# Node-row one-hots of a GNN edge phase: from tensor_scalar to tensor_tensor with a PSUM operand, and behind the copy of places

## The reference, cut to what matters

```python
h = silu(edge_rbf @ W1 + b1)              # per edge, 8 -> 128
weights = h @ W2 + b2                     # per edge, 128 -> 128
node_j = node_feats[col]                  # gather of the neighbour's row
messages = node_j * weights
aggregated = segment_sum(messages, row)   # a later phase here
```

## Time and profile before

| | us |
|---|---|
| median of 3 runs | 8842.73 (8837.77 to 8855.31) |
| the profiled execution | 8818.33 |
| its span on the core | 8816.7 |
| busy: PE / DVE / ACT / POOL | 5016.2 / 3899.3 / 1911.4 / 5309.5 |

### The profile page before, as it was taken

One profiled execution on the slowest core, in us unless ns is written; L12 is line 12 of the kernel. 1 busy time (PEld: TensorE's weight loads), 2 busy tenths in 40 slices (PEclk: granted clock), 3 DMA queues, 4 the chain that ended last, 5 costly groups with the idle time before them and its releaser, 6 DMA issues. The chain is left out here.

```text
span 8816.7 us, 124446 instructions
## 1 busy us (share of the span) xinstructions
PE 5016.2 (57%) x25826; PEld 4198.6 (48%) x25826; DVE 3899.3 (44%) x9651; ACT 1911.4 (22%) x6476; POOL 5309.5 (60%) x5985
## 2 busy tenths in 40 slices
PE   5888888888888888133233332333444444444438
PEld 4777777777777788132222332222322232232234
DVE  6555555555555677233222422232422223223238
ACT  2222222222222001111111111111211212112117
POOL 3556655656656786556666666666366666666651
PEclk7666666666667899566656555555666666666669
DMA  3222222222222686212222122222122222222224
GB/s 104 91 91 95 92 95 91 93 94 95 92 95 93 198 236 211 59 40 47 47 46 47 42 47 47 46 47 47 40 61 59 60 61 59 60 60 60 61 64 155
DMA packets 947475, 711.07 MB, mean 81 GB/s; under 512 B 602499, under 2 KB 811606, under 8 KB 946622
## 3 DMA queue, kind: packets, MB, share of 16 engines
q0 software_dynamic: 163632, 347.28, 13.6%
q1 hardware_dynamic: 245634, 251.14, 9.5%
q10 hardware_dynamic: 538001, 110.77, 6.5%
HBM read 544.79 MB, written 170.29 MB: 81 GB/s over the span
## 5 line engine op out<-in xcount | busy, mean ns | idle before, releaser
L768 POOL DMA_INDIRECT arena<-x1d,edge x3322 | 3148.9, 948 | 1855.5 <-issue 959.2
L1949 PE MATMUL bank<-arena 128*128 x7040 | 1428.4, 381 | 2148.5 <-DVE acc_b L1598 1204.0
L1949 PEld LDWEIGHTS bank<-arena 128*128 128x128 f32 x7040 | 1306.8, 284 | 2338.9 <-issue 2329.0
L707 POOL DMA_INDIRECT msgs<-arena x1664 | 1655.5, 995 | 1242.8 <-DVE arena L1390 764.8
L1592 DVE TENSOR_TENSOR arena<-bank,arena 128x1024 f32<-128x1024 f32 x440 | 537.8, 1223 | 2499.8 <-remote 2090.0
L998 ACT ACTIVATE arena<-edge,arena 128x1 f32 x3520 | 732.0, 282 | 2607.7 <-issue 2057.4
L1598 DVE TENSOR_TENSOR acc_b<-acc_b,bank 128x129 f32 x1760 | 508.5, 289 | 666.1 <-issue 472.2
L1855 PE MATMUL bank<-w2s,acc_b 128*128 128x128 f32 x3328 | 749.9, 394 | 17.0 <-issue 16.5
L1838 PE MATMUL bank<-arena 128*128 (+1 forms) x3328 | 699.6, 363 | 89.3 <-issue 85.1
L1855 PEld LDWEIGHTS bank<-w2s,acc_b 128*128 128x128 f32 x3328 | 636.7, 285 | 161.8 <-issue 161.8
L1838 PEld LDWEIGHTS bank<-arena 128*128 128x128 f32 x3328 | 609.1, 266 | 118.5 <-issue 116.9
(11 more groups left out here) (310 smaller groups left out, 5732.9 us busy)
## 6 DMA issues: line engine op xcount, KB each, us to landing
arena<-rows SPq DMA_DIRECT2D x208, 512.0 KB
arena<-msgs ACTq DMA_DIRECT2D x464, 136.0 KB, 3.3
arena<-msgs SPq DMA_DIRECT2D x464, 136.0 KB, 3.2
arena<-x1d,edge POOLq DMA_INDIRECT x3322
msgs<-arena POOLq DMA_INDIRECT x1664
pred<-arena ACTq DMA_DIRECT2D x98, 256.0 KB
arena<-pred SPq DMA_DIRECT2D x12, 1792.0 KB, 8.8
arena<-xwin SPq DMA_DIRECT2D x208, 64.0 KB
```

The costliest lines, as they stand in the source:

```text
L707: pool.indirect_dma_start(msgs, bass.IndirectOffsetOnAxis(ap=pos[:, b, j:j + 1], axis=0), mrow[:, b, j, :], None).then_inc(scattered[b], 16)
L768: pool.indirect_dma_start(grow_t[:, sl, 0:D], None, x1d, bass.IndirectOffsetOnAxis(ap=edge2[:, odd * RING + sl, 1:2].bitcast(i32), axis=0) ...
L1949: last = mm(sum_at(q, k), oh1[:, q % 2, k, :], grow[:, bass.ds(rows_at[q * TG + k], CW)], start=True, stop=True)
```

## The change

The window one-hots of group g+1 are made by `tensor_tensor` instead of `tensor_scalar`. The second operand is the partition number in one f32 column of PSUM (`number_at`, column 8 of `bank[6]`), broadcast over 8 x 128; it is filled once, ahead of the phase, by a copy of `iota_c`. And the instruction stands behind the copy of places of group g, ahead of the two halves of its messages, no longer between the first scan and the first place product. The first group's one-hots, ahead of the loop, stay where they were.

```diff
-        places_at = bank[6][:, 0:TG]
+        places_at, number_at = bank[6][:, 0:TG], bank[6][:, TG:TG + 1]
...
-                v.tensor_scalar(wsel[:, b], rowsb[:, b, 1, :].rearrange("p (j e) -> p j e", j=TG), iota_c[:, :], None, ALU.is_equal).then_inc(s["wsel_ready"], 1)
+                v.tensor_tensor(wsel[:, b], rowsb[:, b, 1, :].rearrange("p (j e) -> p j e", j=TG),
+                                number_at.rearrange("p (j e) -> p j e", j=1).to_broadcast([P, TG, P]), ALU.is_equal).then_inc(s["wsel_ready"], 1)
...
                     if then:
                         running_counts(ls, 1 - b, 0)
-                        window_onehots(it + b, 1 - b)
                         places_of(ls, g + 1, 1 - b, 0)
...
                     v.tensor_copy(pos[:, b, :], places_at).then_inc(s["pos_ready"], 1)
+                    if then:
+                        window_onehots(it + b, 1 - b)
                     messages(g, b, 0)
...
+            ls.link(v.tensor_copy(number_at, iota_c[:, :]))
             attribute_parts(ls, 0, 0)
```

## The result

The changed kernel took 8939.42 us (median of 4 runs, 8916.06 to 8970.94) against 8840.25 us of the kernel before beside it (4 runs, 8817.72 to 8855.31): a ratio of 1.0116, 95% interval [1.0088, 1.0143], 99 us slower. In a later set of runs (a set is what was measured beside the same executions of the kernel before) the same two kernels took 9001.26 and 8775.11 us, 1.0258 [1.0225, 1.0291]. Slower both times, but the size of the loss differs by a factor of two between the sets. The traces show in which groups the difference lies, and not why.

The account below looks back on a forecast made before the run. Bound: POOL's series of eight scatters plus the path copy, messages, first scatter (13.15 us a group). Only the insertion was priced: 8843 + 118 = 8961 us, other terms nothing; range 8790 to 9200 us.

Parts of the forecast that it names:

- The main step: Edge phase: PE's results come free only when POOL's scatters are through, in almost every group; period 13.15 us.
- first rival: POOL's scatters were held up by the old one-hots; removing them takes 156 us off, to 8805 us; chance 0.21.
- Series plus path: The assumed bound: POOL's eight scatters, 9.97 us, then copy of places, messages and first scatter; sum 13.15 us.
- The form: One-hots on DVE: 756 ns as tensor_scalar become 1.22 us as tensor_tensor with one PSUM operand, bounds 0.76 and 1.4.
- The insertion: One-hots between copy of places and messages: 1.25 us in 5 of 11 groups, 118 us in all; chance 0.52.
- The old place: Between first scan and place product DVE loses 0.76 us per group; nothing gains, as DVE stands 4.0 us anyway.
- PE behind the one-hots: PE's products for the next group start 1 to 2 us later against the messages; costed at nothing.
- SP's queue: Row and attribute loads wait for the later one-hots; DVE may stand up to 2 us at L1375; costed at nothing.
- second rival: PE's answers miss their time and stay held until the series ends: 290 us, 9250 us; chance 0.14.
- POOL's queue: POOL's scatter series: its waits do not change, the series stays 9.97 us; gain 0, at most 54 us.
- The rule that the prediction weighed: On DVE and POOL: 2-port vector instructions and GpSimd exclude each other, normal-mode PSUM ones do not; up to 156 us less.

Follow-up runs that it names:

- c1: The kernel before itself, unchanged, run again for its trace: 8756.3 us, ratio 0.9986 to the kernel before.
- d2: The kernel before plus an idle 1.2 us PSUM-operand comparison behind the copy of places, which then gives the copy's signal: 8895.0 us, ratio 1.0085.
- d1: The changed kernel with the removed tensor_scalar put back idle at its old place; PE still waits for the new one-hots: 9100.7 us, ratio 1.0308.
- c2: The changed kernel itself, run again in a later set: 9001.3 us, ratio 1.0258 to the kernel before.
- e3: The kernel before with only the one-hots' form changed, tensor_tensor with the number from SBUF, at the old place: 7586.5 us, ratio 1.0273.
- c4: The kernel before with its old one-hots one instruction later, behind the first place product: 8744.6 us, ratio 0.9973.
- f1: The kernel before with its one-hots one instruction earlier, ahead of the first scan: 7543.1 us, ratio 1.0208.
- e1: The changed kernel with the one-hots in their old tensor_scalar form, still behind the copy of places: 7479.7 us, ratio 1.0128.

## Why the prediction was right and wrong

The number was right: 8961 us forecast, 8939 measured, period 13.9 forecast and 13.92 in the trace. That it came out so close is luck. The composition was wrong: terms that I had set at nothing were larger than the one I priced, and they partly cancelled. In the later set the same pair lost 226 us, nearly twice the forecast.

- **The main step: PE's results come free when the scatters are through.** The prediction named its own sign of being wrong, results that come free at another time relative to POOL's last scatter, and that sign is there. In the kernel before, the copy of places began 0.99 us behind the end of the series (median; ahead of it in 43 of 207 groups; in c1 0.15 us and 63 groups). In the changed kernel it began 1.90 us ahead of that end, and ahead of it in 130 groups. The messages began 0.99 us behind the end, 1.70 before, and in 65 groups POOL went into the next series after its short pause of 0.30 us, in 18 before. So the first rival's sign (no later than 1.71 us) showed too, though not its cause, since the series had become longer. "Series plus path" describes the kernel before; in the changed one some groups are bound by the series alone and others by PE's late answers.
- **The form.** 1.22 us forecast, 1.212 measured.
- **The insertion**, "mean 5/11 x 1.25 = 0.57 us; over 207 groups 118 us". Mechanism right, size off: 63 us in d2, 0.30 us per group. Part of it is the distance: the one-hots begin 0.08 us behind the copy's start, so the least distance from copy to messages is 1.21 us in the trace, not 1.42. The sample of eleven groups was not at fault. Of all 208 groups of the trace of before, 106 have their messages within 0.25 us of the copy, and raising every distance below 1.21 us to that value adds up to 115 us (96 us in c1). What gave back the rest is not shown.
- **"The old place. Nothing gains."** This failed. That DVE stood 4 us ahead of the copy in the mean does not say that it stood in every group. In the trace of after it went into the copy without a wait (under 0.4 us) in 65 groups, in that of before in 21. Against d1, with the old instruction still there, POOL's idle time is 336 us smaller.
- **"PE behind the one-hots: I cost the shift at nothing under that cover", and "SP's queue: nothing".** Together they failed by 206 us (d1 against d2). The mechanism was in the text as the second rival, at 290 us, with a chance of 0.14; the wait at L1375 had been named, and rose from 65 to 229 us. The rival's sign, copies 17 to 19 us apart, is there: the trace of after has 42 groups with over 17 us between their messages, that of before 16. These groups are also where the two pairs differ: c2 has 71, c1 18.
- **"POOL's queue: the series still 9.97 us."** This failed. I looked at the instruction that is removed and whether it held a scatter. It did not, and the row was no accident: 160 of the 161 scatters that began in it in the trace of before did so in its first 0.1 us, and 159 were let through. Taking it out gained nothing there. I did not look at what its removal does to the instructions behind it. They moved against the scatters, and L707 was busy 206 us longer. The forecast "idle time before the first scatter near 3.7 us" was wrong for the same reason in the other direction: by the group it was 3.13 us before and 2.72 after.

The rule that the prediction weighed (the Trainium skill, SBUF — State Buffer, section "Who interferes with whom") goes on in that section to say that a vector instruction with two SBUF inputs contends with a GpSimd instruction that reads SBUF, and one with at most one such input, outside the 2-port modes, does not. Here the trace agrees on both: scans, products and the one-hots of e3 (two SBUF inputs) held the scatters, 94 of 94 in e3's one-hots; the PSUM form and the messages held 0 of 43 and 0 of 101. The half that the prediction weighed, on tensor_scalar, shows only when a scatter begins well inside the instruction: 116 of 116 in c4, 46 of 46 in f1. I had applied the rule to the moved instruction alone.

Three terms thus make up the changed kernel's loss at this level: the insertion, about 63 us; the late signal, about 206, both measured within one set; and the instruction taken off DVE with the scans' new distance, which together give back between 44 and 170 us. This last is an estimate across sets (1.0308 less 1.0258 or 1.0116, of 8840), because the changed kernel was not measured beside d1 and d2. Why it differs so between two sets of the same kernels stays open.

## What to carry to other kernels

When an instruction leaves a place, ask what its removal does to the timing of the ones that stay, above all where two engines exclude each other and a rhythm happens to fit; the distance between two instructions can be worth more than the instruction. When one that signals is moved, price the signal apart from the work: here the signal's delay cost three times what the added work on the path did (206 us and 63). And a total that comes out right is no proof of the terms; an idle copy of the instruction at the old place and one at the new place, measured beside the change itself, separate most of them.

## What the runs showed of the hardware

**Scatters held by VectorE's instructions.** A GpSimd indirect DMA that begins while VectorE runs a scan ends 0.78 us after it (352 of the 355 that began with over 0.25 us of a scan left, in the changed kernel), in a product or a comparison with both inputs in SBUF 0.84 us after it, and so in the tensor_scalar L1384 when it began more than some 0.1 us into it (116 of 116 in c4). One that began in the first 0.1 us of tensor_scalar was mostly let through (159 of 160 in the trace of before); in the two-input one-hots of e3 0.03 us were enough to be held. VectorE's own instruction is not lengthened: the scans lasted 1271 to 1293 ns in the changed kernel.

**PE's results withheld, in some sets.** The prediction could not say why PE's results came free only behind the scatters. In the sets at 7385 us they do not wait. In e1 ACT evicts the node rows as soon as PE's record ends (1504.37 + 1.92 = 1506.29), in the middle of a series:

```profile
1504.37 1.92 PE L1840 MATMUL bank<-arena 128*128 128x128 f32 x8
...
1505.57 0.97 POOL L707 DMA_INDIRECT msgs<-arena  x1 [0.31 <-issue]
...
1506.40 0.60 ACT L881 ACTIVATE arena<-bank 128x512 f32<-128x512 f32 x1 [0.97 <-PE bank L1840]
1506.52 0.97 PEld L1840 LDWEIGHTS bank<-arena 128*128 128x128 f32 x8
1506.57 1.11 PE L1840 MATMUL bank<-arena 128*128 x8
1506.84 0.97 POOL L707 DMA_INDIRECT msgs<-arena  x1 [0.30 <-issue]
```

The signal of the places comes 0.01 us after the record of their last product there, and 5.4 us after it (median) in the trace of before. It is not the level alone: in the changed kernel, at the same level as before, the median is 1.5 us, and 0.01 us in c2, where 133 of 207 signals came without delay. The level shows in stages that no edit touches, too: POOL's idle time in the later gather stage, L768, is 1016.7 us in e1 and 1855.5 us in the trace of before. So the reading "series plus path" of the prediction holds for the kernel before at one level, and at the other POOL was bound by its series in e1, e3 and f1. What makes the two levels stays open. The records give chip 0 both for the set e (7385 us) and for the set c (8775 us), 12 for d and 15 for f, so the chip's number does not tell them apart; nor do the records say what withholds the results.
